# A selective-scan stage re-tabled: own slot tables for the first and last batch, the skip term computed beside the sums, one function for softplus, six half-states per batch added by transfers

## The reference, cut to what matters

```python
xz = xm @ W_in                        # 512 -> 2 x 1024
xr, z = split(xz)
u = silu(conv4(xr) + b_conv)          # causal, 4 taps, per channel (1024 channels)
x_dbl = u @ W_x                       # 64 + 16 + 16
dt, Bm, Cm = split(x_dbl, [64, 80])
delta = softplus(dt @ W_dt + b_dt)    # 1024 channels x 512 positions
A = -exp(A_log)                       # 1024 x 16 states
h = exp(delta * A) * h + (delta * u) * B      # scan over 512 positions, 16 states
y = sum over the 16 states of h * C
y = (y + u * D_param) * silu(z)
ssm_out = y @ W_out
attn_out = heads @ Wproj + bproj      # heads come from the stage before
out = x + gate * silu(layernorm([ssm_out, attn_out]) @ W_full + b_full)
```

## Time and profile before

| | us |
|---|---|
| median of three runs | 3898.7 |
| the profiled execution, its time | 3902.06 |
| its span | 3899.8 |
| `attend`, from the start of the span | about 1489 |
| first batch's `front`, alone | 1493.5 to 1584.2 |
| scans and sums, 16 halves | 1584.2 to 3810.1 |
| last batch's `tail`, alone | 3810.1 to 3899.8 |

### The profile page before, as it was taken

One profiled execution on the slowest core, in us unless ns is written; L12 is line 12 of the kernel. 1 busy time (PEld: TensorE's weight loads), 2 busy tenths in 40 slices (PEclk: granted clock), 3 DMA queues, 4 the chain that ended last, 5 costly groups with the idle time before them and its releaser, 6 DMA issues.

```text
span 3899.8 us, 36422 instructions
## 1 busy us (share of the span) xinstructions
PE 3364.2 (86%) x12362; PEld 1765.7 (45%) x12362; DVE 2700.1 (69%) x3429; ACT 2043.9 (52%) x3517; POOL 1906.8 (49%) x1147
## 2 busy tenths in 40 slices
PE   7899999999999997668888888888888888888758
PEld 3344444444444433444444444444444444544443
DVE  3253534444353533689898998998998998998981
ACT  2233434343433434746756756756766676676632
POOL 0121221212221221867767757767857867767661
PEclk9999999999999998668998998998998988988859
DMA  5101011010101011012132231232221221221111
GB/s 175 68 1 46 1 46 41 6 46 1 46 1 46 1 76 40 30 52 77 57 111 76 65 129 53 89 111 66 81 98 65 85 94 65 84 98 65 49 62 43
DMA packets 106361, 238.43 MB, mean 61 GB/s; under 512 B 10609, under 2 KB 10721, under 8 KB 103106
## 3 DMA queue, kind: packets, MB, share of 16 engines
q1 hardware_dynamic: 101314, 226.73, 17.1%
q0 software_dynamic: 2304, 8.39, 1.1%
q10 hardware_dynamic: 2560, 0.98, 0.1%
HBM read 193.85 MB, written 33.83 MB: 58 GB/s over the span
## 4 chain that ended last, share of the span: by engine, by line
PE 23%; DVE 21%; ACT 9%; issue 7%; POOL 2%; DMA 0%; POOLq 0%; SPq 0%; DVEq 0%; ACTq 0%
PE bank L1559 12%; DVE HS L1433 9%; DVE acc L1442 8%; PE bank L1574 5%; PE bank L1639 4%; ACT bank L1255 3%; POOL HS L1167 1%; DVE U L1474 1%; PE bank L1637 1%; PE bank L1627 1%; ACT U L1317 1%; PE bank L1583 1%; DVE G L1462 1%; ACT G L1371 1%; ACT L1318 0%
## 5 line engine op out<-in xcount | busy, mean ns | idle before, releaser
L1167 POOL TENSOR_TENSOR HS<-DU,brep 128x1024 f32<-128x1024 f32 x512 | 1198.9, 2363 | 445.0 <-PE bank L1574 443.7
L1433 DVE TENSOR_TENSOR_SCAN HS<-bank,HS 128x1024 f32<-128x1024 f32 x512 | 1168.1, 2284 | 88.7 <-ACT bank L1255 81.0
L1574 PE MATMUL bank<-ident,HS 128*128 128x128 f32 x4096 | 678.9, 317 | 297.9 <-DVE acc L1442 251.5
L1255 ACT ACTIVATE bank<-delta,aneg 128x511 f32<-128x511 f32 x1024 | 662.0, 681 | 410.3 <-DVE HS L1433 409.3
L354 POOL TENSOR_TENSOR PR<-PR,rrec 128x512 f32<-128x512 f32 x256 | 260.0, 1039 | 1160.3 <-DVE rrec L612 1160.3
L1574 PEld LDWEIGHTS bank<-ident,HS 128*128 128x128 f32 x4096 | 555.9, 163 | 574.2 <-DVE HS L1433 324.6
L1442 DVE SCALAR_TENSOR_TENSOR acc<-bank,C,acc 128x512 f32<-128x512 f32 x928 | 647.0, 741 | 101.3 <-PE bank L1574 98.1
L1559 PE MATMUL bank<-XM,w_l 128*128 128x512 f32 x1024 | 509.3, 639 | 54.9 <-DVE U L1474 32.4
L1559 PE MATMUL bank<-w_l,G 128*128 128x512 f32 x1024 | 471.1, 605 | 10.8 <-ACT G L1371 10.8
L441 ACT ACTIVATE PR<-bank,nsmax 128x512 f32<-128x512 f32 x256 | 173.4, 682 | 374.6 <-DVE nsmax L608 374.6
L714 PE MATMUL bank<-w_l,NT 128*128 128x512 f32 x768 | 344.7, 597 | 4.8 <-ACT NT L393 4.8
(11 more groups left out here) (172 smaller groups left out, 3884.4 us busy)
## 6 DMA issues: line engine op xcount, KB each, us to landing
brep<-b_d SPq DMA_DIRECT2D x256, 256.0 KB, 3.2
w_l<-in_L_cond_W_in SPq DMA_DIRECT2D x14, 2048.0 KB, 10.8
w_l<-in_L_cond_W_full SPq DMA_DIRECT2D x8, 2048.0 KB, 8.6
w_l<-in_L_cond_W_out SPq DMA_DIRECT2D x7, 2048.0 KB, 9.0
X<-in_x SPq DMA_DIRECT2D x8, 1024.0 KB, 5.3
x_d<-X SPq DMA_DIRECT2D x8, 1024.0 KB, 4.6
xm_d<-XM SPq DMA_DIRECT2D x8, 1024.0 KB, 3.9
ot_d<-OT SPq DMA_DIRECT2D x8, 1024.0 KB, 5.8
```

The lines of the kernel that those rows point to most:

```text
L1167: nc.gpsimd.tensor_tensor(HS[:, u % DEEP], DU[:, chunks(j, s), :], brep[:, m % 3, :].unsqueeze(1).to_broadcast([P, UC, T]), ALU.mult).then ...
L1255: last = nc.scalar.activation(dA[:, s, i, 1:T], delta[:, c, 1:T], ACT.Exp, scale=aneg[:, c, n:n + 1])
L1433: nc.vector.tensor_tensor_scan(h, dA[:, u % 2].rearrange("p i t -> p (i t)"), h, 0.0, ALU.mult, ALU.add).then_inc(scanned, 1)
L1574: last = nc.tensor.transpose(y_bank[t % 2][:, i * P:(i + 1) * P], h, ident[:])
```

## The change

It has these parts, all in `mix`:

- `SPARED` goes from one state per batch to six: `n` = 3, 6, 9 in `half0` and 4, 6, 9 in `half1`. The terms have a space of their own (`terms`). The two transfers of state `n` are issued in the slots of state `n + 2`.
- Softplus is one activation per chunk (`Softplus`), two chunks between two table loads. POOL keeps only `delta * u`.
- The skip term: ACT writes `u * D` for all eight chunks (`ACT_UD`), POOL multiplies it by `silu(z)` (`gate_skip`), DVE multiplies the turned sum by `silu(z)` and no more, and POOL adds the two (`add_skip`).
- The first batch: its `z` products (`PE_Z_START`) move from before the first scan into slots 12 to 25 of its `half0`, and its `front` no longer waits for the small weights before the first product. `silu(z)` of the first four chunks moves from slot 0 to slot 21.
- The last batch: half of the product with `W_out` (chunks 0 to 3, named `h`) and the whole product with `Wproj` move into slots 10 to 24 of its `half1`. What remains after the last scan is the other half of `W_out`, the addition of the two, and the rest of `tail` in an order of its own, in which transposes and the `W_full` product follow one another tile by tile.
- Nearly all slot numbers of the tables for the other batches change by a few slots.

The diff, cut (tables are shown by two or three lines of theirs):

```diff
-LN_NEAR_1 = "natural_log"
+SOFTPLUS = "softplus"
...
-        SPARED = ((10,), ())
+        SPARED = ((3, 6, 9), (4, 6, 9))
...
-        PE_O = ((2, 2, 2, 3), (5, 5, 5, 5), (14, 15, 15, 15), (21, 21, 22, 22))
+        PE_O = ((2, 2, 2, 3), (5, 5, 5, 7), (14, 15, 15, 15), (21, 21, 22, 22))
...
-        ACT_SILU_Z = {0: (0, 1, 2, 3), 20: (4, 5, 6, 7)}
+        ACT_SILU_Z = {4: (0, 1, 2, 3), 22: (4, 5, 6, 7)}
...
+        POOL_SKIP, POOL_ADD0 = {2: 0, 3: 1, 4: 2, 5: 3, 8: 4, 10: 5, 13: 6, 15: 7}, {2: 0, 3: 1, 4: 2, 5: 3}
+        POOL_ADD1 = {0: 4, 1: 5, 2: 6, 3: 7}
...
+        PE_O_EARLY, ACT_O_EARLY, PE_P_END, ACT_P_END = (10, 12, 14, 16), {11: 0, 13: 1, 15: 2, 17: 3}, ((18, 18), (20, 20), (22, 22), (24, 24)), {19: 0, 21: 1, 23: 2, 25: 3}
+        PE_O_END, PE_CT_END = ((2, 2), (3, 3), (4, 4), (5, 5)), ((6, 6), (8, 8), (10, 10), (12, 12))
...
         def window(j, n):
 
-            later = [m for m in SPARED[j % 2] if m > n]
-            return (later[0], later[0] + 1) if later else (n + 2, n + 2)
+            return n + 2, n + 2 + (n + 2 in SPARED[j % 2])
...
-                            nc.gpsimd.dma_start(acc[:, 2 * k:2 * k + 2, :], scratch_pair(j, k), accum_op=ALU.add).then_inc(summed[k], 16)
...
+                            nc.gpsimd.dma_start(acc[:, 2 * k:2 * k + 2, :], terms[:, 2 * k:2 * k + 2, :], accum_op=ALU.add).then_inc(summed[k], 16)
+
+                def step_times_input(n, c):
                     pool.wait_ge(*ring.done(n, f"dt{c}"))
...
+                    pool.wait_ge(u_done, n * IC + c + 1)
                     nc.gpsimd.tensor_tensor(DU[:, c, :], delta[:, c, :], U[:, c, :], ALU.mult).then_inc(du_done, 1)
 
+                def gate_skip(b, c):
+                    i = b * IC + c
+                    pool.wait_ge(ud_done, i + 1)
+                    pool.wait_ge(z_done, i + 1)
+                    y = (DU if c < HC else G)[:, c, :]
+                    nc.gpsimd.tensor_tensor(y, y, zs(b, c), ALU.mult).then_inc(skip_done, 1)
+
+                def add_skip(b, c):
+                    i = b * IC + c
+                    pool.wait_ge(skip_done, i + 1)
+                    pool.wait_ge(tot_done, i + 1)
+                    nc.gpsimd.tensor_tensor(G[:, c, :], G[:, c, :], DU[:, c, :] if c < HC else zs(b, c), ALU.add).then_inc(g_done, 1)
...
+                def softplus(n, pair):
+                    act.preload_act_table_set(SOFTPLUS)
                     for c in pair:
...
+                        act.wait_ge(ring.full, ring.at(n, f"dt{c}"))
+                        after(act, dA_done, (2 * n + c // HC - 1) * UNITS)
+                        nc.scalar.activation(delta[:, c, :], ring.bank(n, f"dt{c}")[:], ACT.Softplus, bias=col("L1_cond_b_dt", c)).then_inc(ring.emptied["act"], 1)
                     act.preload_act_table_set(EXP_AND_LN)
...
-                        nc.scalar.activation(scratch(j, t), y_bank[t % 2].unsqueeze(1), ACT.Identity, scale=C[:, b % 2, t, n:n + 1]).then_inc(scaled, 1)
+                        nc.scalar.activation(terms[:, t, :], y_bank[t % 2][:], ACT.Identity, scale=C[:, b % 2, t, n:n + 1]).then_inc(scaled, 1)
...
-                        c, y = q * HC + i, y_bank[i % 2][:]
-                        dve.wait_ge(yt_full, j * TURNED + N * TT + i + 1)
-                        if q == 0:
-                            nc.vector.scalar_tensor_tensor(out=y, in0=U[:, c, :], scalar=col("L1_cond_D_param", c), in1=y,
-                                                           op0=ALU.mult, op1=ALU.add).then_inc(tot_done, 1)
-                        else:
-                            dve.wait_ge(ud_done, b * HC + i + 1)
-                            nc.vector.tensor_tensor(y, y, G[:, c, :], ALU.add).then_inc(tot_done, 1)
...
-                        nc.vector.tensor_tensor(G[:, c, :], y_bank[i % 2][:], zs(b, c), ALU.mult).then_inc(g_done, 1)
+                        dve.wait_ge(yt_full, j * TURNED + N * TT + i + 1)
+                        nc.vector.tensor_tensor(zs(b, c) if q else G[:, c, :], y_bank[i % 2][:], zs(b, c), ALU.mult).then_inc(tot_done, 1)
...
+                    if p == B - 1 and s in DVE_O_END:
+                        t = DVE_O_END[s]
+                        dve.wait_ge(ring.full, ring.at(p, f"o{t}"))
+                        dve.wait_ge(*ring.done(p, f"h{t}"))
+                        nc.vector.tensor_tensor(comb[:, t, 0:D], ring.bank(p, f"o{t}")[:], XM[:, t, :], ALU.add).then_inc(ring.emptied["dve"], 1)
```

More of the change, by code:

```diff
@@ L1056, in load_xm @@
                 def load_xm(n):
-                    if n:
-                        for k in range(2):
-                            sp.wait_ge(summed[k], spared(2 * n - 1, 0) * 16)
                     sp.dma_start(XM[:], xm_d[n]).then_inc(xm_in, 16)
@@ L1205, in tail @@
+                    table = of(p, POOL_OUT, POOL_OUT_END)
+                    if s in table:
+                        t = table[s]
                         pool.wait_ge(gate_in, (p + 1) * 16)
@@ L1644, in tail @@
                     attention(p, s + SLOTS)
-                    for t, k in at(PE_O, s):
+                    first = of(p, 0, HC)
+                    for t, k in at(of(p, PE_O, PE_O_END), s):
                         if k == 0:
@@ L1698, in half1 @@
                             front(n, s)
+                        if n is None and s in PE_O_EARLY:
+                            t = PE_O_EARLY.index(s)
+                            pe.wait_ge(g_done, b * IC + HC)
+                            ring.wait_free(pe, b, f"h{t}")
+                            for c in range(HC):
+                                last = nc.tensor.matmul(ring.bank(b, f"h{t}")[:], G[:, c, t * P:(t + 1) * P], wide["out"][:, c, :], start=(c == 0), stop=(c == HC - 1))
+                            last.then_inc(ring.full, 1)
                         attention(b, s)
-                pe.wait_ge(small_in, 3 * 16)
                 pe.wait_ge(ones_done, 1)
```

335 lines of the change are left out of this document (163 added, 172 removed).

## The result

The changed kernel takes 3809.56 us (median of 4 runs, 3807.00 to 3812.81) against 3898.70 us for the kernel before: ratio 0.9771, 95% interval 0.9759 to 0.9782. It is 89.1 us faster. (The 3898.70 us are the median of three runs; a fourth, of 18016 us, is left aside.) The forecast was about 190 us faster, 3710 us, with a range of 3660 to 3775: the sign was right, the size was not, and the range did not hold it.

The account below looks back on a forecast made before the run. DVE was taken to bound the middle, chains through PE both ends. Terms of -33, -9, -108.5, -17, -23 and 0 sum to -190.5 us: 3902.1 to 3711.6, rounded to 3710; range 3680 to 3745, or 3660 to 3775 with two rivals.

Parts of the forecast that it names:

- Term 1: Before the first scan: z products moved away and a shorter softplus chain save 33 us; bounds -25 and -38.
- Term 5: From the last total to the end: less PE work left there saves 23 us; bounds -15 and -30.
- Term 6: Everything before 1493.5 us stays as it is: 0.
- Term 2: First batch's half0: two more spared states and silu(z) out of slot 0 save 9 us; woven-in z products cost only waking the clock.
- rival A: PE's clock stays low where products are woven into the first and last half: +67 us, 3775; chance 0.08.
- Term 3: Middle halves: less DVE work, partly returned as waiting, saves 6.5 us per half0 and 9 per half1, -108.5 in all.
- Term 4: Last half: less DVE work and no final wait for Wproj products, against POOL's skip operations: -17 us; bounds +5 and -25.
- B: Middle halves don't follow DVE's lighter load; PE's in-order queue, transfer waits and POOL's additions take the rest: 3818 us; chance 0.09.
- C: Transfers' landing sets the pace: each of 96 makes DVE wait 3.1 us beyond what was taken: 4008 us; chance 0.04.
- E: Softplus activation takes 3 us more than its neighbours, delaying the first scan and later decays: +100 us, 3810; chance 0.02.
- D: New slots also remove DVE's idle time, 6 us a batch more than said: 3665 us; chance 0.07.

## Why the prediction was wrong, by its own steps

Term 1 (before the first scan, -33): -37.6, near its bound of -38. The way was right, and the first scan came at 1546.6 (1551 forecast).

Term 5 (the end, -23) was right within its bounds: -20.2. The stage takes 69.5 us where I wrote 67. PE's busy time is 52.2, 5 more than my count.

Term 6 (`attend`, 0) holds within 2 us: the first instruction of DVE behind it comes at 1491.92, where the kernel before had it at 1493.55.

Term 2 (first `half0`, -9): -2.0. The step that failed is "they cost nothing while PE runs at full clock". The clock did rise (0.53 to 0.71, so rival A is out). DVE has 4.1 us less work, but its waits came back elsewhere. Its two waits behind the silu at the start of the half (3.12 and 2.32 us) are gone, as forecast; the same silu in slot 21 now makes it wait 2.52, and waits for ACT of 1.4 to 3.1 us have come up in three other places. With half of the contraction of z left out, this half is 6.9 us shorter (117.1 for 124.0): the products are not covered. So of the 4.8 for the silu about 2.9 was kept, and nothing for the products was wrong.

Term 3 (middle halves, -108.5) is the one that failed, and by its sign in `half1`: -34 in all, 74.5 of the 98 us by which the sum missed. DVE's work fell as written. For `half0` I took -6.5 and it was -10.9 on the mean: the two further spared states gave 7.5 us for 5.2 us of sums. For `half1` I took -9 and it was +5.9. The step was: DVE bounds the half, so work off DVE shortens it, less some waiting. The runs put in its place:

- the skip term and softplus, with the slots of before and no spared state: 145.1 to 142.4, -2.7;
- the new slots of `half1`: +5.4 (142.4 to 147.8). About 1.4 of these go with the `Wproj` slots and come back in `half0`; the z readers are none of it. Which of the others made the remaining 4 stays open;
- the heads' load at slot 27: +3 (147.9 to 151);
- three spared states: 0. With the slots of before, +3.5 for the gap of two between 4 and 6, which the new slots hide.

The sum is -2.7 + 5.4 + 3 = +5.7, and +5.9 was measured.

The earlier trace rows could have warned me that a -10.2 can't be kept whole: in `half1` PE was busy for 125.0 us and DVE for 134.4 of 145.1, 9 us apart. They could not have told me that it would be nothing. In the run with the spared states as before, DVE's busy time is 8.1 us above PE's in `half1`, and 7.7 us off it gave nothing (150.35 and 151.0 us); in `half0` it is 6.8 above, and 5.0 off it gave 7.5. I did write that PE's products have less DVE work to lie beside, but I priced it at a few us. The second step missing is the slots: "nearly all slot numbers change by a few slots" has no term in my sum, and its price was 8 us a `half1`, 3 of them by the heads' load. About 2 us come back in `half0` (127.3 with the slots of before, 125.2 with the new ones).

Term 4 (last half, -17): +1.3. The three spared states are the step that failed. I took them at -7.8, and they cost 15: 118.1 without, 132.6 with 3, 6, 9 and 133.0 to 134.8 with 4, 6, 9. Two causes are shown, and they are not the whole: ACT's wait for its scratch space (2.2 us, 134.8 to 132.6 by the edit that removes it) and POOL's skip term (6.0, 132.6 to 126.6). The other 8.5 us above the half without spared states stay open. The rest of the term gave more than I had for it: without spared states the half is 13.6 below 131.7, where I had 17.2 - 7.8 = 9.4.

The rivals. B gave nearly the time (3818), with "the middle doesn't follow", and I gave it 0.09. That is partly luck: the middle gave 34 us, and the other terms gave 23.5 less than B took over from me. Its mechanism was right in part: `half0` followed, and in `half1` it isn't PE's amount of work (11 us less of it gave 1 to 2). C is out: the DVE waits for transfers are 33.1 us in all, some 4 a batch, or under 0.4 a transfer where I took 0.5. But its mechanism stands in the last half, through ACT's scratch space and the late issue. E is out: the softplus activation takes 0.69 us. D did not occur in `half1`, and `half0` gave 4.4 us more than forecast, much as D has it.

The Trainium skill (SBUF — State Buffer, section "SBUF: two separate sides"), on transfers from GpSimd held up by DVE, named in the prediction: the 96 transfers have a median of 5.2 us from issue to landing in place of 4.5, with scans and sums running beside them all the time. Nothing here singles out such a hold-up: the 13 that took over 7 us all had a load from SP's queue in flight beside them, and where the 0.7 us of the median come from no run separates. What cost time was that another engine's buffer hung on the landing, which that rule isn't about.

## What to carry to other kernels

Work taken off the busiest engine is worth what a run says and not what its busy time says: three spared states in place of one gave 7.5 us in `half0`, more than their own 5.0, and three in place of none gave nothing in `half1`, although DVE was busy 7 to 8 us longer than the next engine in both. A cheap run that takes the work off by itself would have told this before the rest was built on it. Before pricing a transfer that takes over work, ask who reuses its source: with one scratch space the next spared state had to wait for its landing (145.9 against 142.3 us a half). And a change of slot tables needs a term of its own: here a load moved close to its product cost 3 us, while the place of a reader in the slot of its product cost nothing on balance. A wait in the timeline is a cause only if removing it moves the time: of the six things I moved to remove one, two did (the heads' load, and the distance between spared states).
